# One block for norm, projections and attention in two of four layers; maxima turned in place; two loads issued earlier

## The reference

```python
xn = layernorm(x)
x = x + attn(xn) + ffn(xn)
```

```python
q, k, v = (split_heads(xn @ W) for W in (Wq, Wk, Wv))
scores = where(causal, q @ k.T, -inf)
attn = softmax(scores / sqrt(8))
out = merge_heads(attn @ v) @ Wo        # + bo in layer 1
```

## Time and profile before

| | before |
|---|---|
| median of 3 runs | 1166.84 us (1166.3 to 1167.66) |
| profiled execution: time | 1165.75 us |
| profiled execution: span | 1163.8 us |
| TensorE busy | 1000.2 us (86%), mean granted clock 0.929 |
| VectorE busy | 783.4 us (67%) |
| ScalarE busy | 641.8 us (55%) |
| GpSimd busy | 384.9 us (33%) |

### The profile page before, as it was taken

How to read it: one execution, slowest core, us unless ns; L and a number is a source line. 1 busy time by engine, 2 the same in 40 slices (tenths; PEclk the granted TensorE clock), 3 DMA queues, 4 the chain that set the end, 5 groups by cost and what they waited for, 6 DMA issues and landing times. The chain is left out here.

```text
span 1163.8 us, 30736 instructions
## 1 busy us (share of the span) xinstructions
PE 1000.2 (86%) x10716; PEld 597.0 (51%) x10717; DVE 783.4 (67%) x1436; ACT 641.8 (55%) x1144; POOL 384.9 (33%) x542
## 2 busy tenths in 40 slices
PE   5389599998949999979699999999988599999696
PEld 2256489883624555447435555445545255554242
DVE  8744145544668899647757777767776788995345
ACT  4712144442627777733276676776646277777364
POOL 2144677772065555660040000000000255555011
PEclk9689699999959999989799999999989699999798
DMA  9678845533833333260000000000017233331002
GB/s 276 216 249 258 269 120 160 148 106 109 270 101 90 106 108 109 79 194 2 1 1 1 0 0 1 0 0 0 0 72 260 77 103 109 109 109 39 1 1 72
DMA packets 166612, 114.19 MB, mean 98 GB/s; under 512 B 15732, under 2 KB 160382, under 8 KB 166546
## 3 DMA queue, kind: packets, MB, share of 16 engines
q1 hardware_dynamic: 161938, 104.40, 29.9%
q0 software_dynamic: 4608, 8.93, 2.2%
HBM read 77.04 MB, written 37.29 MB: 98 GB/s over the span
## 5 line engine op out<-in xcount | busy, mean ns | idle before, releaser
L1669 ACT ACTIVATE at_p<-banks 128x512 f32<-128x512 f32 x384 | 222.8, 597 | 93.2 <-PE banks L1543 89.5
L1685 DVE TENSOR_REDUCE at_mx<-banks 128x12 f32<-128x1536 f32 x128 | 224.2, 1758 | 43.9 <-PE banks L1528 40.9
L1483 POOL TENSOR_SCALAR_AFFINE_SELECT at_p<-at_p 128x512 f32<-128x512 f32 x256 | 160.0, 637 | 162.4 <-ACT at_p L1669 156.3
L1543 PE MATMUL banks<-at_qbl,at_kst 128*128 128x512 f16 x384 | 142.5, 389 | 1.5 <-ACT at_p L1669 1.5
L1475 POOL COPY at_va<-v_all 128x128 f32 (+1 forms) x64 | 16.9, 294 | 305.0 <-PEq L1502 305.0
L1954 PE MATMUL banks<-f_h_hi,w_hi_h 128*128 128x512 f16 x256 | 97.2, 380 | 5.5 <-DVE f_h_lo L2102 3.1
L1955 PE MATMUL banks<-f_h_lo,w_hi_h 128*128 128x512 f16 x256 | 97.0, 379 | 0.0
L1956 PE MATMUL banks<-f_h_hi,w_lo_h 128*128 128x512 f16 x256 | 97.0, 379 | 0.0
L477 POOL DMA_INDIRECT expert_rows<-xn_tok,slot x64 | 64.8, 1013 | 83.5 <-DVE slot L1031 43.0
L1060 DVE TENSOR_TENSOR ex_h_sb<-ex_sg,banks 128x512 f32<-128x512 f32 x56 | 38.2, 688 | 70.6 <-ACT ex_sg L558 43.2
L1521 PE MATMUL banks<-at_ksc,at_qst 32*128 32x128 f16 (+1 forms) x1024 | 47.1, 261 | 40.0 <-DMA at_ksc<-at_k_stacked 17.4
(11 more groups left out here) (419 smaller groups left out, 2357.2 us busy)
## 6 DMA issues: line engine op xcount, KB each, us to landing
xnT<-kernel_padded SPq DMA_DIRECT2D x8, 1024.0 KB, 7.5
at_qst<-at_q_stacked SPq DMA_DIRECT2D x32, 256.0 KB, 3.0
at_ksc<-at_k_stacked SPq DMA_DIRECT2D x32, 256.0 KB, 3.3
at_kst<-at_k_stacked SPq DMA_DIRECT2D x32, 256.0 KB, 2.8
at_qbl<-at_q_stacked SPq DMA_DIRECT2D x128, 64.0 KB, 1.9
expert_rows<-ex_h_sb SPq DMA_DIRECT2D x1, 5760.0 KB, 17.9
gate_up_then_rows<-expert_rows SPq DMA_DIRECT2D x20, 260.0 KB
ssm_powers<-kernel_padded SPq DMA_DIRECT2D x4, 1024.0 KB, 6.2
```

The costliest lines, as they stand in the source:

```text
L1483: pool.affine_select(out=blk, in_=blk, compare_op=ALU.is_ge, fill=0.0, base=0, pattern=[[0, 4], [1, P]], channel_multiplier=-1).then_inc(p ...
L1543: pe.matmul(o, kst[m][:, g, kt * P:kt * P + P], qbl[m][:, g, :, qt * P:qt * P + P], start=True, stop=True).then_inc(t_mm, 1)
L1669: act.activation(dst, k.ps[:, turn_bank(old, g * 3 + n), :].rearrange("p (j q) -> p j q", j=4), ACT.Exp, scale=scale).then_inc(p_ready, 1)
L1685: dve.tensor_reduce(mx[:, :, g * 4:g * 4 + 4].rearrange("p n j -> p j n"), k.ps[:, score_banks(batch, g), 0:3 * P].rearrange("p j (n t) -> ...
```

## The change

`front` no longer opens a block. It returns its five engine programs and some of its semaphores as a `Front`; `attend` opens one block in which each engine runs front's program and then attend's own, with no barrier between. GpSimd sets a semaphore `cleared` after its clears, and every engine waits for that one before its part of attend. What the barrier ordered is now waited for where it is needed: TensorE waits for all of `xT`, 15 subtractions and the set-up of `va` before the first scores, and for the 16th subtraction and the last copy of values before the second group; GpSimd waits for `va`, for the last copy of values and, in layer 1, for the last normalized tile before it adds the bias.

The maxima get one buffer per parity of the batch. The copy to `neg` is gone, the minimum is written back in place, and the transposes read `mx`. VectorE waits, before it overwrites a buffer, until the maxima of the batch before last have been turned, instead of for the minimum of the batch before.

SyncE's loads of `qst` and `ksc` for batches 2 and 3 move from the head of steps 2 and 3 to behind `load_k` in steps 1 and 2. The loop is as it was.

```diff
 def front(...):
-    with nc.Block() as block:
-        @block.gpsimd
-        def _(pool):
-            k.clear_retired(pool)
+    def pool_program(pool):
+        for s in retired:
+            pool.sem_clear(s)
+        pool.sem_inc(cleared, 1)
...
+    return Front(cleared, pool_program, pe_program, act_program, dve_program, sp_program, z_ready, xT_ready, lo_done, v_done)
-def attend(k, at, wo, bo, later=None, prepare=None):
+def attend(k, at, first, wo, bo, later=None, prepare=None):
...
-        mx = k.sb(f"{tag}_mx", [P, 3, HEADS], ctx=st)
-        neg = k.sb(f"{tag}_neg", [P, 2, HEADS], ctx=st)
+        mx = k.sb(f"{tag}_mx", [P, 2, 3, HEADS], ctx=st)
...
             def step(new, mid, old, done):            # SyncE
-                if new is not None and not (isinstance(new[0], int) and new[0] == 0):
+                if new is not None and not isinstance(new[0], int):
                     load_scores(new)
                 if mid is not None:
                     b = b_of(mid)
                     load_k(mid)
+                    if isinstance(b, int) and b < 2:
+                        load_scores((1, b))
                     sp.wait_ge(m_copied, b + 1)
...
+        def pool_program(pool):
+            pool.wait_ge(v_set, 6)
+            pool.wait_ge(first.v_done, NCH)
             if bo is not None:
+                pool.wait_ge(first.z_ready, TILES)
...
             pe.wait_ge(v_set, 6)
+            pe.wait_ge(first.xT_ready, NCH)
+            pe.wait_ge(first.lo_done, 2 * NCH - 1)
             def scores(batch, g):
+                if opening(batch) and batch[1] == 0 and g == 1:
+                    pe.wait_ge(first.lo_done, 2 * NCH)
+                    pe.wait_ge(first.v_done, NCH)
...
-                    ins = pe.transpose(k.ps[0:HEADS, CT_B, qt * P:qt * P + P], neg[:, qt, :], k.ident[:])
+                    ins = pe.transpose(k.ps[0:HEADS, CT_B, qt * P:qt * P + P], mx[:, batch[1], qt, :], k.ident[:])
...
-                if g == 0 and not (isinstance(b, int) and b == 0):
-                    dve.wait_ge(neg_ready, b)
+                if g == 0 and not (isinstance(b, int) and b < 2):
+                    dve.wait_ge(mt_mm, b)
...
-                        dve.wait_ge(mt_mm, b + 1)
-                        dve.tensor_copy(neg[:, 0, :], mx[:, 0, :])
-                        dve.tensor_tensor(neg[:, 1, :], mx[:, 1, :], mx[:, 2, :], ALU.min).then_inc(neg_ready, 1)
+                        second = mx[:, new[1], 1, :]
+                        dve.tensor_tensor(second, second, mx[:, new[1], 2, :], ALU.min).then_inc(neg_ready, 1)
...
+            @block.tensor
+            def _(pe):
+                first.pe(pe)
+                pe.wait_ge(first.cleared, 1)
+                pe_program(pe)
```

More of the change, by code:

```diff
@@ L1 @@
+from collections import namedtuple
 from contextlib import ExitStack
@@ L1238, in front @@
     hi, lo, stored = at.hi, at.lo, at.stored
-    with nc.Block() as block:
-        def z_of(t):
-            return k.z8[:, t % 8, :] if z_out is None else z_out[:, t, :]
-        @block.gpsimd
-        def _(pool):
-            k.clear_retired(pool)
[L1248 to L1256, removed]
-                if c >= 2:
[L1258 to L1356, removed]
@@ new lines, in z_of, with pe_program, project @@
+    def z_of(t):
+        return k.z8[:, t % 8, :] if z_out is None else z_out[:, t, :]
+    def pool_program(pool):
+        for s in retired:
+            pool.sem_clear(s)
+        pool.sem_inc(cleared, 1)
+    def pe_program(pe):
+        def project(c):
+            xc = k.xT[:, c * CHUNK:(c + 1) * CHUNK]
+            pe.wait_ge(xT_ready, c + 1)
+            for n, (bank, w) in enumerate(((Q_B[c % 2], wq), (K_B[c % 2], wk))):
+                if c >= 2:
+                    pe.wait_ge(lo_done, (c - 2) * 2 + n + 1)
+                pe.matmul(k.ps[:, bank, :], w[:], xc, start=True, stop=True).then_inc(qk_mm, 1)
+            if c >= 2:
+                pe.wait_ge(v_done, c - 1)
+            for t in range(TPC):
+                ins = pe.matmul(k.ps[:, V_B[c % 2], t * P:t * P + P], k.xT[:, c * CHUNK + t * P:c * CHUNK + t * P + P],
+                                wv[:], start=True, stop=True)
+            ins.then_inc(v_mm, 1)
+        for c in range(NCH):
+            if c >= 2:
+                pe.wait_ge(xT_ready, c - 1)
+            for t in range(c * TPC, c * TPC + TPC):
+                pe.wait_ge(z_ready, t + 1)
+                pe.transpose(k.ps[:, T_B[c % 2], t % TPC * P:t % TPC * P + P], z_of(t), k.ident[:]).then_inc(turned, 1)
+            if c:
+                project(c - 1)
+        project(NCH - 1)
@@ new lines, in act_program, with evacuate @@
+    def act_program(act):
+        if not aggregated:
+            act.wait_ge(aggr_done, TILES)
+        act.activation(std[:], mv[:, :, 1], ACT.Sqrt, bias=k.eps[:, 0:1]).then_inc(std_done, 1)
+        def evacuate(c):
+            for n, bank in enumerate((Q_B[c % 2], K_B[c % 2])):
+                act.wait_ge(qk_mm, c * 2 + n + 1)
+                if c >= HB:
+                    act.wait_ge(stored[c % HB], c // HB * 64)
+                act.activation(hi[:, c % HB, n, :], k.ps[:, bank, :], ACT.Copy).then_inc(hi_done, 1)
+            act.wait_ge(v_mm, c + 1)
+            act.activation(k.v[:, c * TPC:c * TPC + TPC, :], k.ps[:, V_B[c % 2], :].rearrange("p (t c) -> p t c", c=P),
+                           ACT.Copy).then_inc(v_done, 1)
+        for c in range(NCH):
+            act.wait_ge(turned, c * TPC + TPC)
+            act.activation(k.xT[:, c * CHUNK:(c + 1) * CHUNK], k.ps[:, T_B[c % 2], :], ACT.Copy).then_inc(xT_ready, 1)
+            if c:
+                evacuate(c - 1)
+        evacuate(NCH - 1)
@@ L2445, in layer3 @@
             at = Heads(k, "at3", a)
-            front(k, at, z, w["a3q"], w["a3k"], w["a3v"], False)
-            attend(k, at, w["a3o"], None)
+            first = front(k, at, z, w["a3q"], w["a3k"], w["a3v"], False)
+            attend(k, at, first, w["a3o"], None)
         global_net(k, beta)
@@ L2473, in layer1 @@
         at = Heads(k, "at1", a)
-        front(k, at, None, w["a1q"], w["a1k"], w["a1v"], True)
+        first = front(k, at, None, w["a1q"], w["a1k"], w["a1v"], True)
         rows_set = k.sem("stacked_rows_set3")
@@ L2481, in next_weights @@
             sp.wait_ge(arrived, 16 * len(weights))
-        attend(k, at, w["a1o"], w["a1bo"], next_weights, lambda pool: dequantize(pool, k))
+        attend(k, at, first, w["a1o"], w["a1bo"], next_weights, lambda pool: dequantize(pool, k))
     def last_weights(sp):
```

93 lines of the change are left out of this document (81 added, 12 removed).

## The result

The changed kernel takes **1155.07 us** (median of 4 runs, 1151.06 to 1155.91) beside 1166.57 for the kernel before: a ratio of 0.9893, 95% interval 0.9869 to 0.9918. Forecast were 1150.6 and a range of 1145 to 1157.5. The direction and the range held; the gain is 11.5 us where 16.2 were expected. The profiled execution took 1155.18 us, its span is 1153.1.

A forecast was written before the change was run, and what follows sets the result against it. VectorE was taken to pace the attention loop, with holes in each opening. Terms 9.45 + 0.3 + 1.6 + 3.9 + 1.0 = 16.25 off 1165.75 gave 1149.5, on the runs' footing 1150.6 us; range 1145 to 1157.5.

The forecast's parts named there:

- Seam: Between front and attend, layers 1 and 3: without the barrier first maxima start 5.05 and 4.4 us sooner, together 9.45.
- TensorE's additions: Head of attend's TensorE program: semaphore additions taken as done early; rival, only after the last matmul: 1152.9 us, chance 0.09.
- Maxima in place, opening: Openings of both attention layers: removing the copy between maxima saves 0.15 us per layer, 0.3 in all.
- Cost nothing: GpSimd's bias addition in layer 1, from 318.9: first mask still in time with 1 us of cover, so no cost.
- Copy in the loop: Attention loop: about 0.08 us won per batch before the scores bind, at 20 of 32 batches, 1.6 us.
- the slower rival: Loop: SyncE's chain from scores to next ksc costs 1.5 us per batch, up to 1187 us; chance 0.02.
- The upper bound of 0.29 per batch: Loop: the removed copy comes back whole at 28 batches, 8.1 us; as a rival 1144 us, chance 0.08.
- the page of the Trainium skill that the prediction weighed there: "VectorE: DVE Perf Modes": minimize VectorE operations; by it each removed copy's whole 0.29 us would come back.
- Loads of batch 2: Third batch of both layers: earlier loads shorten VectorE's hole by 1.6 and 2.3 us, together 3.9; qbl next late.
- The chain grows: Rival: the store of maxima comes through only behind the earlier loads, 1.4 us more in layer 1; 1152 to 1154.5, chance 0.11.
- Batch 3: Fourth batch: earlier loads remove 1.0 of TensorE's 1.32 us wait in layer 3; layer 1 shows no such wait.
- The footing: Whole kernel: the sum starts from one profiled execution, 1165.75 us, then moves up by 1.09 to the runs' median, 1166.84.

The follow-up runs named there:

- one block alone: The kernel before with only the barrier replaced by waits for single events, old load order and copy kept; 1158.47 us, ratio 0.9920.
- all loads early: The changed kernel with SyncE's loads of the scores' operands a step earlier for every batch, in the loop too; 1151.63 us, ratio 0.9836.
- bias early: The changed kernel with GpSimd's layer 1 bias addition ahead of its wait for the copied values; 1156.99 us, in a second run 1153.94.
- loads alone: The kernel before with only the loads of batches 2 and 3 a step earlier, barrier and copy kept; 1162.92 us, ratio 0.9952.

## Why the prediction was right, and where it fell short

*Seam.* Right in mechanism and size, 9.38 of 9.45. First scores came as soon as the 15th subtraction was done, in layer 3 too, where the prediction had TensorE's own last matmul bind (the two end within 0.1 us there); TensorE's additions had run ahead, as the drain of the earlier trace rows had said, and that rival falls. By the earlier trace rows it would have left 3.2 in layer 3 rather than the 3.4 that the prediction has; nothing hangs on it.

*Maxima in place, opening.* The step that failed is the one that put GpSimd's addition at "Cost nothing". It was followed on GpSimd's own queue to the first mask, and not beside VectorE. The rows were there: an addition of 8.82 us that starts with maxima of 6.75 ends 2 us behind them, and the minimum reads two blocks of `mx` in SBUF. The Trainium skill's page "SBUF — State Buffer", section "Who interferes with whom", says that a VectorE instruction with two SBUF inputs contends with a GpSimd instruction that reads SBUF, and calls the contention an exclusive lock, in which the order of issue decides who waits. The runs agree: 1.77 to 2.45 beside one long addition, always to its end, 0.37 beside short ones, 0.17 to 0.27 with it out of the way. The copy of one block alone has one SBUF input and was held as well (2.10), which that sentence doesn't cover. The term came to -1.24 in place of 0.3.

*Copy in the loop.* The mechanism held: a batch takes 9.70 instead of 9.78, by the 0.08 that the scores of the earlier trace rows leave. The count was off. With the shorter batch SyncE's chain, which the prediction had named only as the slower rival, binds now and then, 9.83 to 9.89, and half of the term is lost; with all loads early it is not. The upper bound of 0.29 per batch falls, and with it, as far as this loop goes, what the page of the Trainium skill that the prediction weighed there would have given.

*Loads of batch 2.* 3.85 of 3.9, with qbl next late, as said. That the size fits so well is in part luck: by the same steps the changed kernel's other two profiled executions give 5.2 and 4.4.

*The chain grows.* This rival, which the prediction gave 0.11, did not show in the changed kernel, but not because its mechanism is missing. GpSimd's hold on the minimum, which the prediction did not have, put layer 1's first store at 328.57, when `ksc` was nearly in; in layer 3 it was nearly in as well, and in the loop the loads still stand behind the store. With the bias early, or all loads early, the store lands only behind the loads. The prediction's price for it, 1.4 us on the chain in layer 1, is near the 0.9 to 1.8 more that this store takes in the kernels with the minimum not held to the end of the long addition.

*Batch 3:* 0.99 in layer 3, as forecast, but layer 1 lost 0.52, for which the prediction had no term; loads alone lost 0.40 there. VectorE's third maximum of batch 2 stood 0.59 us before and stands 1.10 now. TensorE's clock is back at the full level about 4.5 us behind the batch's first maximum, where it was 2.7. Here are the first 5.8 us of batch 2's maxima, before and after:

```profile
341.20:347.00 5.80, 5.33 (x80) 2.26 (x82) 4.07 (x3) 3.84 (x8) 2.98 (x6) 0.76 0.15 40
```

```profile
335.60:341.40 5.80, 5.54 (x73) 2.30 (x71) 3.56 (x3) 3.45 (x7) 2.96 (x6) 0.61 0.33 92
```

The granted clock is 0.61 where it was 0.76, and VectorE busy 3.56 where it was 4.07: the batch that now starts sooner meets more of the 1.2 GHz level. No run changes the clock alone, so that this is the cause is read from the rows and not shown.

*The footing.* By the two profiled executions the gain fell 5.7 us short of the sum, and 2.66 of this lie outside the two attentions: the sum was made against one execution, which was better than the others in a stretch that the change doesn't touch. The move up by 1.09 to the runs' median had allowed for a part of it, so the forecast itself was 4.5 us too low. By ratios the change is worth 0.9891, 0.9893 and 0.9903 in three places, some 11 to 13 us.

What stays open: whether the early loop batches' late landings are due to the instruction packets, why batch 3 lost in layer 1, and how much of the bias edit's 1.7 us is real.

## What to carry to other kernels

When a barrier goes, list what now runs at the same time that did not before, and look at each pair of VectorE and GpSimd instructions that both read SBUF; a 0.2 us operation can inherit the length of its neighbour. A chain that has just enough slack for a loop's batch takes back what a faster batch wins, so move it with the edit. Loads that are moved ahead of a small store make that store land behind them, so look at what waits for the store. And take the sum's footing from several executions, stage by stage, when single stages differ by 2 us between runs.

## What the runs showed of the hardware that was not expected

VectorE's small operations with SBUF operands, the copy too, stood for up to 2.45 us beside one GpSimd addition, while its reductions out of PSUM ran on beside the same addition at 6.75 for four, as in layer 3 without it. The wait shows as a longer operation, not as idle time before it: a mean by groups hides it. A store of 8 KB that takes 1.38 us by itself landed 0.15 to 0.25 us behind loads that SyncE had issued ahead of it, 107 times of 107, after up to 4.84 us. Loads of `ksc`, 3.3 us in the median, took over 4.5 only where an instruction packet started while they were under way.
